# Cross-attention with values in four column tiles, pair sums on GpSimd and keys placed by DMA; grouped attention with the tail turned first

## The reference

```python
x = x + xattn(layernorm(x), ctx, Wq_d, W_qk, Wkv_d, Wv_u)
x = x + attn(layernorm(x), ..., k_cache, v_cache, block_idx)
x = x + ffn(layernorm(x), w1, mean_w1, w2, mean_w2, w3, mean_w3)
# xattn: 16 heads of 32, 1601 context keys in each batch
C_kv = K @ Wkv_d                                   # 1601 x 32
CqWqk = (Q @ Wq_d @ W_qk).reshape(b, n, 16, 32)
attn = softmax(einsum('bnhl,bkl->bhnk', CqWqk, C_kv) / sqrt(32))
out = einsum('bhnk,bkhd->bnhd', attn, (C_kv @ Wv_u).reshape(b, nkv, 16, 32))
# attn: 32 query heads over 8 key heads of 128; 512 cached keys and 64 new ones
# ffn: W = base + mean(|w - base|) * sign(w - base) for w1, w2, w3
```

## Time and profile before

| | |
|---|---|
| three runs | 1060.43, 1057.27, 1057.63 us; median 1057.63 |
| the profiled execution | 1058.74 us, span 1057.0 us |
| mean granted TensorE clock | 0.959 |
| busy in the span: PE, DVE, ACT, POOL | 974.6 (92%), 651.4 (62%), 478.4 (45%), 293.0 (28%) us |
| cross-attention | about 36 to 370 us of the span |
| rotated keys | 370 to 400 us |
| grouped attention | 400 to 919 us |
| feed-forward | 919 to 1057 us |

### The profile page before, as it was taken

The page is one execution under the profiler, slowest core; times in us unless marked ns, Lnnn a source line. Parts: engine busy times, 40 slices in busy tenths (PEclk is TensorE's granted clock), DMA queues, the critical chain, the costliest instruction groups (busy, mean ns, idle before and its releaser), DMA issues. The chain is left out here.

```text
span 1057.0 us, 15125 instructions
## 1 busy us (share of the span) xinstructions
PE 974.6 (92%) x5018; PEld 678.0 (64%) x5018; DVE 651.4 (62%) x1166; ACT 478.4 (45%) x843; POOL 293.0 (28%) x243
## 2 busy tenths in 40 slices
PE   4689999999999897999999999999999997789998
PEld 2344545554444266777777877777777785568886
DVE  3474666667565154757757576675757665388883
ACT  3203444344434455635535364563535544154551
POOL 3343033213300003323323233232323323144330
PEclk9767999999989999999999999999999999879999
DMA  8255523541700062101111010110102000166531
GB/s 310 105 229 229 229 73 158 229 171 64 248 10 1 1 239 90 40 21 41 41 38 41 20 40 20 40 40 20 40 20 60 11 1 0 53 216 208 181 120 40
DMA packets 40413, 98.69 MB, mean 93 GB/s; under 512 B 8626, under 2 KB 10674, under 8 KB 39346
## 3 DMA queue, kind: packets, MB, share of 16 engines
q1 hardware_dynamic: 38994, 98.01, 26.3%
q10 hardware_dynamic: 1376, 0.13, 0.1%
HBM read 97.08 MB, written 1.05 MB: 93 GB/s over the span
## 5 line engine op out<-in xcount | busy, mean ns | idle before, releaser
L1216 POOL TENSOR_TENSOR head_probs<-head_probs,inverse_den 128x576 f32<-128x576 f32 x128 | 146.8, 1147 | 412.4 <-DVE inverse_den L1147 412.2
L721 DVE TENSOR_REDUCE max_part<-psum 128x1 f32<-128x400 f32 (+2 forms) x256 | 133.2, 567 | 74.8 <-PE psum L594 74.7
L699 ACT ACTIVATE probs<-psum 128x1024 f32<-128x1024 f32 (+1 forms) x104 | 106.3, 1023 | 113.1 <-PE psum L614 113.1
L1094 ACT ACTIVATE head_probs<-psum,neg_max 128x576 f32<-128x576 f32 x128 | 94.5, 738 | 76.8 <-PE psum L991 43.1
L1160 DVE TENSOR_REDUCE neg_max<-psum 128x1 f32<-128x576 f32 x128 | 96.2, 754 | 36.3 <-PE psum L975 28.9
L625 PE MATMUL psum<-probs,c_nat 128*64 128x512 f32 (+1 forms) x416 | 114.0, 627 | 1.5 <-ACT probs L699 0.6
L1140 DVE TENSOR_TENSOR probs_t_low<-psum,probs_t_high 128x512 fp32r<-128x512 f32 x128 | 86.6, 681 | 7.9 <-ACT probs_t_high L1100 7.9
L975 PE MATMUL psum<-k_high,query_t_high 128*128 (+1 forms) x256 | 86.4, 337 | 4.9 <-DVE query_t_low L1125 2.9
L594 PE MATMUL psum<-c_t,q_now 96*128 96x400 f32 (+1 forms) x256 | 83.7, 403 | 5.8 <-DVE c_t L671 3.2
L990 PE MATMUL psum<-ident,head_probs 128*128 128x128 f32 x512 | 78.0, 275 | 3.8 <-DVE mixed_t_low L1185 2.0
L614 PEld LDWEIGHTS psum<-q_now,c_t 97*128 97x128 f32 (+1 forms) x208 | 31.5, 189 | 76.4 <-ACT probs L699 53.5
(11 more groups left out here) (163 smaller groups left out, 1944.0 us busy)
## 6 DMA issues: line engine op xcount, KB each, us to landing
cache<-in_ctx_dram SPq DMA_DIRECT2D x4, 3202.0 KB, 14.3
ctx_t_odd<-in_ctx_dram SPq DMA_DIRECT2D x4, 3202.0 KB, 15.2
w_raw<-in_L_ffn_w_dram SPq DMA_DIRECT2D x24, 448.0 KB, 5.0
w_raw<-in_L_ffn_mean_w_dram SPq DMA_DIRECT2D x24, 448.0 KB, 5.8
ffn_raw<-in_L_ffn_w_dram SPq DMA_DIRECT2D x42, 256.0 KB, 3.9
ffn_raw<-in_L_ffn_mean_w_dram SPq DMA_DIRECT2D x42, 256.0 KB, 4.1
wq_nat<-in_L_attn_wq_dram SPq DMA_DIRECT2D x32, 256.0 KB, 2.8
wo_nat<-in_L_attn_wo_dram SPq DMA_DIRECT2D x32, 256.0 KB, 2.7
```

The costliest lines, as they stand in the source:

```text
L699: act.activation(probs[slot % 2][0:rows, :].rearrange("p (a n) -> p a n", a=2), psum[0:rows, score_bank(back, slot):score_bank(back, slot) ...
L721: dve.tensor_reduce(max_part[:, qt, piece:piece + 1], psum[:, MAX_BANKS[i % len(MAX_BANKS)], 0:width], AX.X, ALU.max).then_inc(s_max, 1)
L1094: act.activation(probs[:, qt, :].rearrange("p (a k) -> p a k", a=2), psum[:, 2 * (qt % 2):2 * (qt % 2) + 2, 0:HALF], ACT.Exp, bias=neg_max ...
L1216: pool.tensor_tensor(probs[:, qt, :], probs[:, qt, :], rden[:, qt:qt + 1].to_broadcast([P, KEYS]), ALU.mult).then_inc(s["norm"], 1)
```

## The change

Cross-attention is written anew; the loops are unrolled.

- **Values.** `c_nat` has 32 columns, no ones. Two key tiles make a unit (7 units, the last of one tile), and a unit issues four products: tile and half of the heads at partitions 0, 32, 64 and 96 of bank 4. Sums of odd and even tiles stay apart until the mix, whose weights `wv_u` hold Wv_u twice.
- **Denominators.** GpSimd adds the probabilities of the two tiles of a unit (`add_pair`, 128 x 1024, six a step). TensorE multiplies these sums by ones, two sums at a time, in four column tiles of bank 5, behind units 3, 5 and 6. Probabilities have four buffers, and so have sums. An exponential waits until the buffer, four tiles back, is used by values and by GpSimd.
- **Keys.** ScalarE makes the high part `c_high` from `c_parts`, VectorE the low part `c_low`, and SP places them in `c_t` with 15 DMAs of a batch. The stack, its 13 transposes, their copies, `c_stage`, and GpSimd's stack work are gone. VectorE copies `natural` straight to `c_nat`. Queries are read from `q_t` in place.
- **Banks.** Scores have two pairs (0 and 1, 2 and 3). Compress, natural and maxima go through a ring of two banks, 6 and 7, in a fixed order; each item waits for the one two places ahead to be read.
- **Mix** of a batch is issued in the next step, behind compress; VectorE's update of x stands behind `c_low` and ahead of that step's first maximum. ScalarE copies the denominators, VectorE the values.
- **SP's order** in a batch: place keys, context two ahead, (in the last but one: the cache gather), weight pieces of the next batch.
- **Grouped attention**: ScalarE and VectorE do the tail ahead of the fourth tile; the mix waits for the tail and the high parts, later for the values' low parts, and for the probabilities' low parts only ahead of its last four products. The second tail product runs over 128 rows, of which half are zeros.

```diff
+UNITS = (KT + 1) // 2
+DENS = UNITS // 2
+SCORE_BANK = (0, 2)
+U_BANK, DEN_BANK = 4, 5
+RING = 6
+DEN_AT = {3: 0, 5: 1, 6: 2}
+ABS_AT = {3: 0, 4: 1, 5: 2}
...
+    if lead is None and prep is None:
+        kinds = ("",) * UNITS
+    elif lead is None:
+        kinds = ("c", "n") + ("",) * (UNITS - 2)
+    elif prep is None:
+        kinds = ("mmmm", "mmmmm", "mmmmmm", "mmmmmm", "mmmmmm", "mmmmm", "")
+    elif lead == 0:
+        kinds = ("mmmmmm", "mmmmmm", "mmmmc", "mmmmn", "mmmmmm", "mmmmmm", "")
+    else:
+        kinds = ("cmmmm", "nmmmmm", "mmmmmm", "mmmmmm", "mmmmmm", "mmmmm", "")
...
+            def place_keys(b):
+
+                sp.wait_ge(s_chi, b + 1)
+                sp.wait_ge(s_clo, b + 1)
+                wait(sp, s_sb, KT * (b - 2))
+                for row, part in ((0, c_high), (LKV, c_low), (2 * LKV, c_high)):
+                    for g in range(GROUPS):
+                        sp.dma_start(c_t[row:row + LKV, b % 3, g * MAIN:(g + 1) * MAIN].bitcast(F32),
+                                     part[g * LKV:(g + 1) * LKV, 0:MAIN].bitcast(F32)).then_inc(s_ct, 16)
+                    sp.dma_start(c_t[row:row + LKV, b % 3, FULL * P:NCTX].bitcast(F32),
+                                 part[0:LKV, MAIN:MAIN + TAIL].bitcast(F32)).then_inc(s_ct, 16)
...
+            def add_pair(b, u):
+
+                pool.wait_ge(s_exp, KT * b + 2 * u + 2)
+                wait(pool, s_den, DENS * b + 1 if u >= 4 else DENS * b)
+                pool.tensor_tensor(sums[u % 4][:, :], prob_buffer(b, 2 * u)[:, :], prob_buffer(b, 2 * u + 1)[:, :],
+                                   ALU.add).then_inc(s_add, 1)
+
+            for back, lead, prep in STEPS:
+                for u in range(UNITS - 1):
+                    if back is not None:
+                        add_pair(back, u)
+                    if prep is not None and u < 3:
+                        difference(prep, u)
...
+                for half in range(2):
+                    cols = slice(half * BANK, (half + 1) * BANK)
+                    for odd, t in enumerate(tiles):
+                        at = 2 * LKV * half + LKV * odd
+                        mm = pe.matmul(psum[at:at + LKV, U_BANK, :], c_nat[0:rows_of(t), b % 3, t, :],
+                                       prob_buffer(b, t)[0:rows_of(t), cols],
+                                       start=(u == 0), stop=(t + 2 >= KT))
...
+                for u in range(UNITS):
+                    items = ring[u]
+                    if u == 0 and back is not None:
+                        if prep is not None:
+                            send(items[:1])
+                            items = items[1:]
+                        if back > 0:
+                            mix(back - 1)
+                    if back is None:
+                        send(items)
+                        continue
+                    if 2 * u + 2 < KT:
+                        scores(back, 2 * u + 2)
+                    send(items[:2])
+                    if 2 * u + 3 < KT:
+                        scores(back, 2 * u + 3)
+                    send(items[2:4])
+                    values(back, u)
+                    if u == UNITS - 1 and lead is not None:
+                        turn_max(lead)
+                    if u in DEN_AT:
+                        denominators(back, DEN_AT[u])
+                    send(items[4:])
+                if back is None and lead is not None:
+                    turn_max(lead)
                 if lead is not None:
+                    scores(lead, 0)
+                    scores(lead, 1)
+            mix(BATCH - 1)
...
+                ring = ring_of(lead, prep)
+                for u in range(UNITS):
+                    items = ring[u]
+                    if u == 0 and back is not None:
+                        if prep is not None:
+                            receive(items[:1])
+                            items = items[1:]
+                        if back > 0:
+                            update_x(back - 1)
+                    if u in ABS_AT and prep is not None:
+                        abs_sum(prep, ABS_AT[u])
+                    receive(items)
...
             def mix(last):
 
                 pe.wait_ge(s["taill"], last + 1)
+                pe.wait_ge(s["th"], TT * (last + 1))
+                for t in range(ST):
+                    pe.matmul(psum[:, 6, :], value[0][:, t, :], probs_t[0][:, t, :], start=(t == 0), stop=False)
+                pe.matmul(psum[:, 6, :], value[0][:, ST, :], probs_t[0][:, ST, :], start=False, stop=False)
                 pe.wait_ge(s["vl"], 2 * ((last // REP) + 1) if isinstance(last, int) else vl_at[0])
...
                 if last:
 
+                    act.wait_ge(s["pt"], TT * n)
+                    act.activation(probs_t[0][0:SEQ, ST, :], psum[0:SEQ, 6, :], ACT.Copy).then_inc(s["tailh"], 1)
                     turned_high(g, i, TT - 1)
-                    act.activation(probs_t[0][0:SEQ, ST, :], psum[0:SEQ, 6, :], ACT.Copy).then_inc(s["tailh"], 1)
...
                 if last:
-                    turned_low(g, i, TT - 1)
                     dve.wait_ge(s["tailh"], n)
                     dve.tensor_tensor(probs_t[0][SEQ:P, ST, :], psum[0:SEQ, 6, :], probs_t[0][0:SEQ, ST, :],
                                       ALU.subtract).then_inc(s["taill"], 1)
+                    turned_low(g, i, TT - 1)
```

532 lines of the change are left out of this document (259 added, 273 removed).

## The result

The changed kernel takes **1083.6 us** (median of four, 1077.7 to 1094.5) where the kernel before takes 1057.7: slower by a ratio of 1.022, 95% interval 1.015 to 1.029. Forecast were 1052 and, for the range, 1018 to 1078. The three executions behind that number spread over 11 us, so a size taken from it can be up to 10 us too small. The profiled execution, 1094.5 us at a clock of 0.917, is 6 to 17 us longer than they are.

The account below looks back on a forecast made before the run. TensorE's stream was taken to set the steady step, with waits for maxima replacing it after the change. Cross-attention +13.5 and grouped attention -19 made -5.5 on 1058.7, 1053, and 1052 us as median; range 1018 to 1078.

Parts of the forecast that it names:

- the clock: Steady cross-attention steps: falls to half clock behind sparse TensorE work, 1.1 us a step, bounds 0 to 3.5.
- Grouped attention: Grouped stage: with the tail first, TensorE's wait ahead of the head mix goes; gain 19 us, bounds 14 and 20.
- the mix no longer waits: Grouped attention: TensorE's 20.2 us of waiting for the tail's low part in 32 mixes falls to near zero.
- zero rows: 0: Grouped attention: making one product 128 rows high at the same columns costs or gains 0.
- TensorE's work: Steady cross-attention step: TensorE's own work after the change adds up to 29.1 us.
- rival (b): Cross-attention: waits overlap better than in the walk, a steady step is 33 us; total 1012; chance 0.20.
- The walk: Steady cross-attention step followed through the two-bank ring: 37.5 us against 36.7, with 8.4 us of waiting.
- The shared read: Steady step: GpSimd's two-operand reads hold VectorE's low part or sum into x; +2.0 us, 0.7 to 2.6.
- The first exponential step: Cross-attention's first step with exponentials: cold compress, no update of x; change 0.
- First maxima: Step of cross-attention's first maxima: 0.6 to 0.67 us each with two banks at half clock against 0.49; +4 us.
- Last steps: End of cross-attention: the step without prep -5 us and the last step -5 us.
- (a): Cross-attention: clock falls in every steady step for 10 us, low part always loses the port; +18, 1070; chance 0.28.

Follow-up runs that it names:

- cross_only: The changed kernel with grouped attention as before, so the cross-attention half alone: 1106.1 us, ratio 1.048 to the kernel before.
- g_only: The kernel before with the whole change of grouped attention and none of the change in cross-attention: 1029.8 us, ratio 0.973.
- x_best: x_free_abs with the five copies of batch 0's second high band issued by ScalarE and not by SP: 1025.5 us.
- x_free_abs: The changed kernel with low part taken from PSUM, addition to x at the next step's end, absolute sums behind their unit's fourth maximum: 1026.3 us.
- x_nolock: The changed kernel with GpSimd's two-operand operations (pair sums, weight differences) replaced by copies of one operand: 1068.6 us.
- x_abs: The changed kernel with only the absolute sums moved, from ahead of their unit's maxima to behind the fourth: 1053.5 us.
- x_last: x_best with the last batch's weight pieces issued ahead of the gathers and the first absolute sums behind maxima: 1020.5 us.
- x_order_abs: x_abs with reciprocal, mixed and unit 0's maxima also put ahead of the low part and the addition to x on VectorE: 1053.3 us.
- x_delay: x_best with seven unread VectorE reductions ahead of unit 0's first maxima in five steps: 1048.1 us.
- x_delay_fill: x_delay with TensorE computing 20 unread products of 512 columns where it would sit idle: 1040.4 us.

## Why the prediction was wrong

It was wrong in sign and 31.6 us too low (26.8 against 1078.8); the measured time is past the end of the range. The step that failed is the clock: I had it cost 1.1 us a steady step and at most 3.5, from one fall behind unit 0, and the traces show two or three falls a step that cost 3.6 (cross_only) to 7.6. The two steps at the front and the last but one add to it, and a gain in grouped attention that I had priced at 0 hid 12 us of the miss. By its steps, sizes in us of the profiled execution:

- **Grouped attention**, -19 forecast, -30.8 (g_only by medians -27.3). The step "the mix no longer waits" was right: 15.7, inside 14 to 20, since 3.1 of the waits stay. The step that failed is "zero rows: 0". They give 11.8. The row was to be had: L1005's 0.50 us beside 0.39.
- **TensorE's work**, 29.1 per step. At full clock the best steps of x_best are 35.3, with TensorE shown busy in 33.8. The products have the prices I gave them (a unit of four-column values 1.0 from start to start, two maxima 0.47 where a bank is free). What is over are short waits for a ring bank, which show at the weight loads and not at the products; in the five steps of x_free_abs (total, times, longest):

```profile
PEld psum L588 <- DVE max_part L756: 45.8, 105, 1.1
```

  So even at its best the new cross-attention saves 1.3 us of 36.7 per step, and rival (b), 33 a step, was out of reach.
- **The walk**, 37.5. It had TensorE wait 2.1 us in unit 0 without the shared read and 4.1 with it; measured are 2.0 (x_nolock) and 4.77. It also had the late units 3 to 5 short of a bank behind the absolute sums (0.56, 0.56 and 1.02). x_nolock tests the sum: its steady steps are 44.3 in the mean with 13.7 us at 1.2 GHz in most, and with those taken out at 0.47 us each they come to some 37.6, an estimate. The mechanism and the size were right. (7.85, 0.65 and 1.85 add up to 10.35, not to the 10.45 of the walk; it changes nothing.)
- **The shared read**, +2.0 within 0.7 to 2.6. Low part +1.75 and addition +1.03 in the step shown: 2.8, which is also the difference of the waits (4.77 and 2.0). Slightly over my bound, because I let only the low part lose.
- **The clock**, +1.1 within 0 to 3.5: here the size failed. I allowed one fall per step, behind unit 0. The step shown has three, 17 us at 0.50 in all, a step of cross_only two, 10 us (44.55 at clock 0.89). Taking out the time in which TensorE was idle anyway (0.8 and 2.5 us) and pricing the rest at the 0.47 above, they cost 7.6 and 3.6 us, an estimate. The walk, the read and this make 47.9 and 43.9, against 47.9 and 44.6 measured: it closes within 0.7. My bound took "10 us at half, less the slack" for the whole of it. Over five steps the miss is 13 to 32 us.
- **The first exponential step**, 0 forecast, +5.5 (+1.0 in cross_only). The difference of the two is mostly the clock's: 23.4 us at 0.50 here, 11.5 in cross_only, 9.5 in the kernel before. GpSimd does wait 4.93 us for a weight piece in it (4.46 in cross_only), but its difference is done long before VectorE's absolute sum asks for it, and nobody waits for that. x_abs takes 8 us off this step, 3.7 if cross_only's 41.1 is the measure.
- **First maxima**, +4, measured +9.3, and they begin 2.4 later on top. Placing took 0.62 us per copy in SP's queue, not the 0.48 of the gathers, so 9.5 us and the first product at 57.05. Within the stage the low part of batch 1 was held (1.61 and 2.09 us), an absolute sum stood behind it, and TensorE waited 5.4 us for the maxima behind both.
- **Last steps**, -5 and -5: +2.0 and -3.9. The step without preparation is at 38 us with a clock of 0.83, like its predecessor of the earlier trace rows at 0.86; I had put 1.7 us for contention and clock there. x_last has 30.7, at clock 1.00.
- **Rivals.** (a), with its 1070, was the case that came: the clock falls in each step and the read is lost. It was itself too cheap, by the second and third fall and the two steps at the front. The length that I took as its condition, a low stretch of some 4.5 us, is not borne out: in x_nolock the clock falls behind a wait of 2.0 us. I gave it 0.28 with the forecast at 0.42, and the range's end was built from one fall. The chance of slower, 0.37, belonged higher: my own walk said 8.4 us of waiting and let them cost 1.1 beyond themselves.

## What to carry to other kernels

When an edit makes TensorE's work sparser, look for every stretch in which it will wait, the repeated waits of half a microsecond too, and count the work behind each at half clock: a fall costs about half its length where TensorE has work throughout, less where it is idle anyway. An operation with two SBUF operands on VectorE should not be placed by order around a busy GpSimd but freed of one operand (PSUM) or put where GpSimd rests, and an operation that waits for a load should stand behind what TensorE waits for, unless the next load waits in turn for it (the 6.2 us of x_last). And a product whose height differs from its neighbours' is a price of its own at each occurrence.

## What the runs showed of the hardware

- A product of 64 rows among those of 128 costs 0.37 us more per occurrence than one of 128 rows with zeros (11.8 us by 32), at the same number of columns.
- While GpSimd reads two operands without a gap, each two-operand operation of VectorE on SBUF lasts until one of GpSimd's ends, even one of 0.21 us (2.09, x_order_abs). Operations with one operand, or one of two in PSUM, keep their length beside it (absolute sum 1.08, low part from PSUM 0.56).
- The granted clock went to 0.50 in each steady step with a stall of 5 us (x_delay), and in none when 20 unread products filled it (x_delay_fill). Such a stall is not needed: it also fell where TensorE waited 2.0 us (x_nolock) and in late units with waits of 0.56 to 1.02 (cross_only), and now and then with 0.6 (x_best).
- What a fall costs: 1.6 us for 3.4 us at half clock where TensorE has work (steps of x_best and x_last), 1.5 to 1.7 for 6.8 where it is idle in the first 2 to 3 of them (x_delay).
- A copy from SBUF to SBUF holds SP's queue for 0.62 us per issue, a gather from memory for 0.48.
